# Layer 1's finished rows of a graph network: scale on ScalarE and bias on GpSimd, or both in one VectorE instruction

## What is computed

```python
h = x @ W;  e_src = h @ a_src;  e_dst = h @ a_dst
e = leaky_relu(e_src[src] + e_dst[dst], 0.2)
w = exp(e - segment_max(e, dst)[dst])
z = segment_sum(w, dst)
out = segment_sum(h[src] * (w / z[dst])[:, None], dst) + b
h1 = relu(out)          # layer 2 starts from this
```

## Time and profile before

| | us |
|---|---|
| median of 3 runs | 1469.35 |
| lowest, highest | 1468.12, 1650.85 |
| the profiled execution | 1466.84 |
| its span, first to last instruction | 1465.1 |
| TensorE busy in it | 1379.4 (94%) |
| VectorE busy in it | 1131.0 (77%) |
| ScalarE busy in it | 911.7 (62%) |
| GpSimd busy in it | 433.7 (30%) |

### The profile page before, as it was taken

One profiled execution on the slowest core, in us unless ns is written; L12 is line 12 of the kernel. 1 busy time (PEld: TensorE's weight loads), 2 busy tenths in 40 slices (PEclk: granted clock), 3 DMA queues, 4 the chain that ended last, 5 costly groups with the idle time before them and its releaser, 6 DMA issues.

```text
span 1465.1 us, 25470 instructions
## 1 busy us (share of the span) xinstructions
PE 1379.4 (94%) x8952; PEld 1318.3 (90%) x8952; DVE 1131.0 (77%) x1540; ACT 911.7 (62%) x1601; POOL 433.7 (30%) x336
## 2 busy tenths in 40 slices
PE   2996999999999999899999999999998999999997
PEld 2995988999999999899999999999998997799996
DVE  5888998836998634677878868788678888788885
ACT  6886777322485321648758478476687321799995
POOL 1000000000000010525736356364477310455453
PEclk9997999999999999999999999999999999999999
DMA  7001000221344610000000000000011496467641
GB/s 204 9 1 43 12 23 24 72 109 58 118 126 158 197 36 0 23 1 23 0 0 22 0 4 18 0 22 0 0 33 55 118 314 154 132 163 171 171 99 21
DMA packets 49077, 100.21 MB, mean 68 GB/s; under 512 B 7230, under 2 KB 23365, under 8 KB 48990
## 3 DMA queue, kind: packets, MB, share of 16 engines
q1 hardware_dynamic: 40801, 75.05, 16.4%
q0 software_dynamic: 7488, 22.26, 7.4%
q10 hardware_dynamic: 701, 1.79, 0.4%
HBM read 68.25 MB, written 33.70 MB: 70 GB/s over the span
## 4 chain that ended last, share of the span: by engine, by line
PE 66%; DVE 5%; DMA 3%; issue 2%; ACT 1%; POOL 1%; POOLq 0%; SPq 0%; ACTq 0%; DVEq 0%
PE ps L444 12%; PE ps L445 12%; PE ps L446 12%; PE ps L982 5%; PE ps L1027 4%; PE ps L1006 4%; PE ps L1029 4%; PE ps L1028 4%; PE ps L1008 4%; DMA hin<-hid_d 1%; PE ps L1451 1%; POOL prlo L1214 1%; DVE mcol L1251 1%; DVE prlo L1214 1%; PE ps L753 1%
## 5 line engine op out<-in xcount | busy, mean ns | idle before, releaser
L1214 POOL TENSOR_TENSOR prlo<-prob,prhi 125x500 fp32r<-125x500 f32 x180 | 258.8, 1446 | 249.8 <-ACT prob L1152 249.1
L1251 DVE TENSOR_REDUCE mcol<-ps 125x1 f32<-125x1250 f32 x120 | 174.9, 1457 | 74.0 <-PE ps L982 72.4
L1150 ACT ACTIVATE prhi<-ps 125x500 fp32r<-125x500 f32 x300 | 176.6, 589 | 71.3 <-PE ps L1008 64.4
L1027 PE MATMUL ps<-prhi,vhi 125*128 125x250 f32 x600 | 171.9, 286 | 12.4 <-POOL prlo L1214 8.1
L1152 ACT ACTIVATE prob<-ps 125x500 f32<-125x500 f32 x300 | 176.3, 588 | 1.7 <-DVE prlo L1214 1.7
L1029 PE MATMUL ps<-prlo,vhi 125*128 125x250 f32 x600 | 168.4, 281 | 0.0
L1028 PE MATMUL ps<-prhi,vlo 125*64 125x250 f32 x600 | 167.3, 279 | 0.0
L1006 PE MATMUL ps<-qst,kst 128*125 128x250 f32 x600 | 156.3, 284 | 3.1 <-issue 1.3
L1008 PE MATMUL ps<-q,k 128*125 128x250 f32 x600 | 153.8, 280 | 0.0
L444 PE MATMUL ps<-hhi,pthi 125*125 125x384 f32 x400 | 153.2, 383 | 0.0
L1755 POOL MEMSET q<- 128x2500 f32 x1 | 2.2, 2184 | 485.9 <-PE ps L446 485.9
(11 more groups left out here) (354 smaller groups left out, 3851.0 us busy)
## 6 DMA issues: line engine op xcount, KB each, us to landing
w1all<-in_L_ffn_W_dram SPq DMA_DIRECT2D x8, 1152.0 KB, 11.9
w2st<-in_L_ffn_W_dram SPq DMA_DIRECT2D x8, 1152.0 KB, 6.5
wqst<-in_L_ffn_Wqkv_dram SPq DMA_DIRECT2D x12, 384.0 KB, 4.3
hid_d<-tin SPq DMA_DIRECT2D x10, 375.0 KB
hin<-hid_d SPq DMA_DIRECT2D x10, 375.0 KB
vtin<-xn_d SPq DMA_DIRECT2D x10, 375.0 KB
out_dram<-accr POOLq DMA_DIRECT2D x10, 375.0 KB, 8.1
xres<-in_x_dram SPq DMA_DIRECT2D x10, 336.0 KB
```

What stands on the lines that cost most here:

```text
L1027: pe.matmul(ps[:, b:b + GQ], vhi[:, e, kt, :], hi, start=kt == 0, stop=False)
L1150: act.activation(prhi[:, n % RING, :], bank(3 + n % 3, P, 2 * GQ), ACT.Exp, scale=float(HD) ** -0.5)
L1214: eng.tensor_tensor(prlo[:, n % RING, :], prob[:, n % 3, :], prhi[:, n % RING, :].bitcast(f32), ALU.subtract)\
L1251: dve.tensor_reduce(mcol[:, e, t:t + 1], ps[0:P, 0:N], AX.X, ALU.max, negate=True).then_inc(sem("max"), 1)
```

## The change

VectorE's one instruction for each finished tile becomes two on other engines.

- ScalarE reads the sum out of PSUM, times the reciprocal, into `tin` (new `finish1` in ScalarE's list, slot 4 of the turn in place of slot 9) and raises `agg_read`.
- GpSimd adds the bias `brow` in place in `tin` and raises a new semaphore `row_biased`. SyncE's stores, and its load of the second bias, wait for that one.
- VectorE keeps the reciprocal, which moves to slot 15 of the turn in which the tile's weights are made (`reciprocal1`, just ahead of `lower`), with waits that its place needs.
- Three further edits belong to it: `v_row` of the later value rows becomes part of `row_biased`, the first `lower2` waits for a semaphore that VectorE raised itself some steps before, and `brow_in` is waited for on GpSimd.

The core of the diff:

```diff
         def lower2(dve, t):
+            if t == 0:
+                dve.wait_ge(sem("src_parts"), KD)
...
             def row_out(t):
-                sp.wait_ge(sem("agg_read"), t + 3)
+                sp.wait_ge(sem("row_biased"), t + 1)
...
             row_out(9)
-            sp.wait_ge(sem("agg_read"), T + 2)
+            sp.wait_ge(sem("row_biased"), T)
             sp.dma_start(brow[:, :], bcast(gb2)).then_inc(sem("brow_in"), 16)
...
             pool.sem_inc(sem("wq_lo"), 1)
+            pool.wait_ge(sem("brow_in"), 16)
+            for t in range(T):
+                pool.wait_ge(sem("agg_read"), t + 3)
+                pool.tensor_tensor(tin[:, t % 2, :], tin[:, t % 2, :], brow[:, :], ALU.add).then_inc(sem("row_biased"), 1)
...
+            def finish1(t):
+
+                u = t % 2
+                act.wait_ge(sem("agg_sum"), t + 3)
+                if t >= 2:
+                    act.wait_ge(sem(f"g1_out{u}"), 16 * (t // 2))
+                act.activation(halves(tin[:, u, :]), two(4 + 2 * u, P, HALF), ACT.Copy, scale=zsum[:, u, 5:6])\
+                    .then_inc(sem("agg_read"), 1)
...
                 for t in range(T):
+                    if g == turn_at(t + 1, 4):
+                        finish1(t)
                     if g == turn_at(t - 1, 9):
                         higher(act, 0, t)
...
-            def finish1(t, u):
-
-                if t == 0:
-                    dve.wait_ge(sem("brow_in"), 16)
+            def reciprocal1(t):
+
                 if t >= 2:
-                    dve.wait_ge(sem(f"g1_out{u}"), 16 * (t // 2))
-                dve.scalar_tensor_tensor(halves(tin[:, u, :]), two(4 + 2 * u, P, HALF), zsum[:, u, 5:6],
-                                         halves(brow[:, :]), ALU.mult, ALU.add).then_inc(sem("agg_read"), 1)
+                    dve.wait_ge(sem("agg_read"), t + 1)
+                dve.wait_ge(sem("agg_w"), t + 1)
+                dve.reciprocal(zsum[:, t % 2, 5:6], wsum[:, t:t + 1])
...
-                        if g == turn_at(t + 1, 9):
-                            ending(dve, order, 0, t, finish1)
                         if g == turn_at(t - 1, 15):
+                            reciprocal1(t)
                             lower(dve, 0, t)
```

More of the change, by code:

```diff
@@ L676, in v_turn @@
                 pe.wait_ge(sem("tile_lo"), 2 * T + t + 1)
-            pe.wait_ge(sem("v_row"), t + 1)
+            pe.wait_ge(sem("row_biased"), T + t + 1)
             for k in range(KD):
@@ L723, in v_affine @@
             dve.wait_ge(sem("v_scaled"), t + 1)
-            dve.tensor_tensor(vtin[:, u, :], vtin[:, u, :], lnrow[:, 1, :], ALU.add).then_inc(sem("v_row"), 1)
+            dve.tensor_tensor(vtin[:, u, :], vtin[:, u, :], lnrow[:, 1, :], ALU.add).then_inc(sem("row_biased"), 1)
         diag0 = tin[:, :, :].rearrange("p a c -> p (a c)")
@@ L1755, in _ @@
             order.did(pool.memset(q2[:, :, :].bitcast(f32), 0.0))
-            pool.wait_ge(sem("v_row"), T)
+            pool.wait_ge(sem("row_biased"), 2 * T)
             order.did(pool.memset(k2[:, :, :].bitcast(f32), 0.0))
```

## The result

| | before | changed |
|---|---|---|
| median, us | 1468.61 (18 executions) | 1471.48 (18 executions) |
| profiled execution, us | 1466.84 | 1471.60 |
| its span, us | 1465.1 | 1469.9 |
| mean granted clock | 0.987 | 0.988 |

The changed kernel takes 1.0022 times as long, with an interval of 1.0014 to 1.0029: slower by 3 us, far inside the 2% that were called the same. One of before's 18 executions was in a slower state (1650.85 us) and is not in the ratio. The two profiled executions differ by 4.8 us. Before's lies 1.8 us under its median and the changed one's on it; that is why this pair shows more than the medians.

A forecast was written before the change was run, and what follows sets the result against it. TensorE, busy 94% of the span, was taken as the bound. Terms 0 + 0 + 0.3 + 0.5 + 1.2 + 1.0 + 0.8 = +3.8 us over 1468.1, rounded to 1472; range 1464 to 1479, likeliest 1469 to 1475.

The forecast's parts named there:

- Removal, 0: Layer 1's aggregation: taking ten 1017 ns instructions off VectorE gives TensorE close to nothing, 0; bound 4.1 us.
- ScalarE, 0: ScalarE's queue in layer 1: ten new PSUM reads, 0.9 us each, delay `pthi` without cost, 0; upper bound 0.9 us.
- Reciprocal, +0.3: Hand-over to layer 2: the reciprocal ahead of `lower` of tiles 8 and 9 adds 0.16 us twice, 0.3 us.
- The hold of 1.8 us an instruction: Counting stage: each GpSimd add holds a VectorE instruction with two SBUF inputs for 1.8 us; bounds 0 and 2.3.
- Only `lower` and the unpacking are not: Counting stage: most VectorE instructions have two SBUF inputs and can be held by an add; `lower` and unpacking are not.
- First four tiles, +0.5: First four tiles of layer 1: holds cost VectorE 2.4 us, mostly swallowed by its waiting; 0.5 us for TensorE.
- Tile 4, +1.2 and +1.0: Tile near 233 us: the add holds `ohs`, 1.2 us more, making a 3.2 us wait; then the clock falls, 1.0 lost.
- Hand-over, +0.8: Hand-over to layer 2: tile 7's add holds VectorE's staging-buffer reads, putting off the next weights load by 0.8 us.
- the last two adds find VectorE waiting or on `lower2`: 0: End of the hand-over: the last two adds meet VectorE waiting or reading PSUM, so they cost 0.
- Hidden in full: Rival: GpSimd's adds meet `lower` or idle VectorE, so only removal counts: 0 to -4.1 us, 1464 to 1468; chance 0.27.
- Holds at most tiles: Rival: VectorE becomes slower engine in counting stage, holds reach TensorE: +9 to +11 us, 1477 to 1479; chance 0.2.
- Over 2% slower: Rival: every add makes a wait over 2.2 us followed by lasting half clock: 29 us or more; chance 0.02.

The follow-up runs named there:

- the first experiment: The changed kernel with GpSimd's ten bias adds left out, only raising the semaphore (layer 1's bias missing): 1467.75 us, ratio 1.0001 to before.
- the repeat: The changed kernel itself, unaltered, measured again on the same chip beside other runs: 1472.76 us, ratio 1.0039 to before.
- only the hand-over moved: The changed kernel with the adds of tiles 7 and 8 moved off the second weights' slices and `row_in(2)` ahead of `row_out(8)`: 1469.78 us, 1.0008.
- second: The kernel before, VectorE still finishing tiles, with GpSimd adds alone on unused data after each of the first seven sums: 1472.23 us, 1.0033.
- third: The changed kernel with GpSimd's adds put off until VectorE stands at `lower`, tile 8's until the last weight slice is split: 1472.53 us, 1.0042.
- fifth: The changed kernel with only tile 4's add put off until VectorE stands at `lower`: 1470.51 us, 1.0011.
- ninth experiment: The changed kernel, all adds placed: tiles 0-5, 7 beside `lower`, 8 behind the last slice, 6 unmoved; `row_in(2)` ahead of `row_out(8)`: 1467.82 us, 0.9999.

## Why the prediction was right, and where it wasn't

The forecast was 1472.0 us, and 1471.48 was measured; +3.8 us over 1468.1, against +2.9 between the medians. The likeliest case was given as 1469 to 1475, the whole range as 1464 to 1479. The mechanism, holds by GpSimd's adds at tile 4 and in the hand-over, was the one that the runs showed. That the sum came so near is in part luck. In the pair of traces the holds and the clock put TensorE 7.8 us behind before until the third row of layer 2, twice the forecast sum, and 3.6 us of it came back at a place that the prediction doesn't have. Term by term:

**Removal, 0: right as a sum.** The add left out gives 1.0001 and all adds placed 0.9999. With GpSimd writing only it is 0.9984, a gain of 2 us, within the bound of 4.1 (which left out the 0.5 us for `packed`). But the 0 is made of two parts in the trace of the first experiment. TensorE loses 1.4 us by the start of the third row, mostly to a fall of the clock, and gains 2.1 where before waits for a row at 325.88. In all nine traces in which ScalarE finishes the tiles that wait is 0.6 us or less; with VectorE finishing and the adds alone it is there, 2.38 us. So it goes with the change and not with lateness; by what, no run shows. The three traces differ in one thing that would fit: behind the wait of 2.0 us at tile 4 the clock stayed at 1.00 in the last one and fell in the two others, to 0.50 in 236 to 239 us (add left out) and to 0.57 in 238 to 241 (all placed). That this is the whole difference is argued, not shown.

**ScalarE, 0: right.** `pthi` never became late; its waits shrank from 8.8 to 7.4 us (150 to 330 us; the 12.9 that the prediction divided by seven tiles has one of 4.1 us from before the stage). It did use some of this slack: see `packed` below.

**Reciprocal, +0.3:** too small to be seen; the add left out, which has the moved reciprocal too, puts it together with ScalarE's part at 1.0001 times the time, at most 1.0014.

**The hold of 1.8 us an instruction: near where it is met in full, too high in the mean.** A single `ohs`, forecast near 2.5 us, took 2.45, 1.65 more than usual. VectorE's busy time in the stage says about 12 us for ten adds; the forecast took 14.4 for eight. The last add met nothing, and the one at 269.61 fell on a short `ohs` of 0.48 that was already running.

```profile
163.84 2.35 POOL L1736 TENSOR_TENSOR tin<-tin,brow 125x768 f32<-125x768 f32 x1 [155.32 <-ACT tin L2019]
164.41 2.45 DVE L2371 TENSOR_TENSOR ohs<-iota,scodd 128x1252 bf16<-128x1252 f16 x1
...
166.96 0.33 PE L1904 MATMUL ps<-ohs,ohd 128*125 128x313 bf16 x1 [0.86 <-ACT packed L2026]
```

**"Only `lower` and the unpacking are not" held: wrong.** The unpacking of counts, one SBUF input, took 2.12 us under the add at tile 4, 1.6 more than usual, and again 2.10 to 2.13 us in the repeat, with two adds, and with only the hand-over moved. With tile 4's add moved away the unpackings of that tile took 0.57 at the most, and one of tile 5's was held instead (2.15). Under the writes the longest was 0.58. The step failed because its rows show only two-input instructions and one from PSUM, and nothing with one SBUF input. (The one from PSUM wasn't wholly under GpSimd's instruction, as the prediction says: it ended at 1094.22, GpSimd's at 1093.96. `lower` then bore it out, with its usual 1.18 us under every add placed beside it.) The Trainium skill ("SBUF — State Buffer", section "Who interferes with whom") has instructions with two SBUF inputs and a reading GpSimd instruction exclude one another; the trace agrees for `ohs`, the slices and their lengths. That sentence doesn't cover the held unpacking.

**First four tiles, +0.5: measured +0.9**, by another way than thought. It wasn't an `ohs` that came late, but `packed`: the held `ohs` of tile 0 delays the counting turn, and TensorE then waits until ScalarE has read the counts out of PSUM (0.86 us, above). The buffers did swallow the rest: three more adds move the marks by 0.1.

**Tile 4, +1.2 and +1.0: measured +2.8 together** (the marks go from 0.9 to 3.7). The add came at 234.55, not 233.7: ScalarE's instruction began at 233.59, since the turn was 0.9 us late. It met the unpacking instead of `ohs`, and the hold on the path was 1.55 us. So the wait is 3.57, not 3.2 us. The clock behind it:

```profile
238.00:241.00 3.00, 3.00 (x15) 2.87 (x15) 2.12 (x3) 2.22 (x7) 0.00 (x0) 0.58 0.30 93
```

0.58 for 3 us, which costs about 1.3 us (3 times 0.42) beside the 1.55. The forecast of the fall was right; the split behind it, that a wait of 2.0 us leaves the clock alone, isn't: waits of 2.02 to 2.04 us were followed by 0.50 to 0.57 in five kernels (the first, second, third, fifth and ninth experiment; in the second 0.57 in 240 to 243 us) and by 1.00 in two (before, and GpSimd only writing).

**Hand-over, +0.8: too low; +2.5 at the row wait and +4.1 with the half clock behind it, then partly given back.** Tile 7's add was seen rightly (`wjunk` 2.56 us). The step that failed is "the last two adds find VectorE waiting or on `lower2`: 0". Tile 9's did; tile 8's fell on the last slice, 299.79, since the whole chain ran late by then; both together put tile 1's row load off by 6.2 us, 3.75 of which were there before. From the fifth tile on 3.6 us of this come back: before has a wait of 2.2 us at 325.88 and half clock behind it, and the changed kernel meets neither. One late load took the place of another; the prediction had no term for this.

**Rivals.** *Hidden in full* fell with 1.0014 as the lower end of the ratio; its time is that of the kernel in which all adds are placed. *Holds at most tiles* fell: only tiles 0 and 4 and the hand-over let them through. It begins to be true with two adds a tile (six waits, +9 us). *Over 2% slower* was never near: the clock fell once in the counting stage, and once in the hand-over, to 0.63 in 308 to 311 us.

**What stays open.** Whether the unpacking was held as an instruction that reads and writes SBUF, or for another trait of its form (uint16, strided), wasn't tried. Nor is it known why before's wait at 325.88 goes with the change, or what made the kernel with all adds beside `lower` as slow as it was. The pair of profiles ends 4.8 us apart and the medians 2.9; 0.7 us of what comes between arises near 370 us, in layer 2's aggregation, and no run here pins it down.

## What to carry to other kernels

Here ten instructions moved from VectorE, 10.2 us, cost it 12 us of holds, since what took their place on GpSimd reads SBUF: count the hold, not the instruction, and look at what VectorE issues at the very time when the moved one starts. An engine that is 92% busy, as VectorE in the stretch from 182 to 246 us, need not be what the end waits for: find what ended each wait of the bounding engine, and give the relief a value only where the removed instruction stands ahead of it. And before a store or a load is put off "because nobody waits for it", read which transfers stand behind it in its queue.

## What the hardware showed that was not expected

- Both sides of a hold stretch. An add that began 0.65 us before the end of a two-input VectorE instruction took 2.35 us; the one that met none took 1.80. The VectorE instruction that began under it took up to 2.6.
- An instruction of 0.52 us with one SBUF input, unpacking 125x313 uint16, took 2.12 us when it began 0.05 us into an add, and 0.56 in the mean beside GpSimd's memsets.
- A GpSimd instruction that only writes (2.06 us of memset) didn't lengthen VectorE's at all: 776 against 773 ns. It was itself lengthened beside the unpackings, from 1.86 us to 2.31 and 2.78.
- The granted clock fell to between 0.50 and 0.57 in some 3 us behind waits of 2.02 to 2.04 us in five kernels, and stayed at 1.00 behind waits as long in two. A prediction can't set the edge finer than "about 2 us".
- Two adds a tile cost 3 to 6 us more than one; seven adds on which nothing depends cost 5 us. Their price is set by what they fall on, not by what waits for them.
